# MetaFormer block, 16 images of 128 x 32 x 32: the first image taken in halves up to its first K, the second weight scale moved to round 1, the statistics of image 1 moved behind the maxima of image 0

## The reference

```python
x = x + _L0_conv_ref(_ln_c(x), w_qkv, w_out, b_out)   # attention on the normalised image
t = _to_tokens(x)
t = t + _L0_ffn_ref(_ln_t(t), Wr, br, W1, ..., Wo, bo)
...
    k = jax.nn.softmax(k, axis=-1)                    # over the 1024 pixels
    context = jnp.einsum('bhdn,bhen->bhde', k, v)
    out = jnp.einsum('bhde,bhdn->bhen', context, q)
...
    w = jax.nn.softmax(jnp.mean(x, axis=0) @ Wr + br, axis=-1)
    h = relu(_bn(x @ W1 + b1, g1, be1, m1, v1))       # per expert
    h = relu(_bn(h @ W2 + b2, g2, be2, m2, v2))
    return einsum(h @ Wo + bo, w)
```

## Time and profile before

| | us |
|---|---|
| median of 3 runs (lowest, highest) | 821.94 (819.64, 822.42) |
| profiled execution | 819.77 |
| its span | 818.0 |
| PE busy | 791.9 |
| POOL, DVE, ACT busy | 578.8, 525.6, 443.5 |

### The profile page before, as it was taken

The page is one execution under the profiler, slowest core; times in us unless marked ns, Lnnn a source line. Parts: engine busy times, 40 slices in busy tenths (PEclk is TensorE's granted clock), DMA queues, the critical chain, the costliest instruction groups (busy, mean ns, idle before and its releaser), DMA issues.

```text
span 818.0 us, 12728 instructions
## 1 busy us (share of the span) xinstructions
PE 791.9 (97%) x4186; PEld 669.9 (82%) x4186; DVE 525.6 (64%) x999; ACT 443.5 (54%) x560; POOL 578.8 (71%) x497
## 2 busy tenths in 40 slices
PE   6999999999998799999999999999999999999997
PEld 5998999999987678888888888888888888888885
DVE  4688777877865446665665656656656566565663
ACT  2576767767675554554554545545455455454542
POOL 5558788787857168667766776777777776677665
PEclk9999999999999889999999999999999999999999
DMA  7124344343342160210101201102022020110100
GB/s 240 53 79 161 123 163 147 112 170 128 131 154 103 54 231 1 78 65 13 77 26 51 77 0 77 54 23 77 1 77 77 0 77 26 51 77 0 51 26 26
DMA packets 22107, 64.52 MB, mean 79 GB/s; under 512 B 2608, under 2 KB 6840, under 8 KB 22080
## 3 DMA queue, kind: packets, MB, share of 16 engines
q1 hardware_dynamic: 22080, 64.19, 21.4%
HBM read 38.98 MB, written 25.20 MB: 78 GB/s over the span
## 4 chain that ended last, share of the span: by engine, by line
PE 64%; ACT 1%; DVE 0%; POOL 0%; POOLq 0%; issue 0%; DVEq 0%
PE psum L552 63%; PE psum L505 1%; PE psum L621 0%; POOL xn_lo L1045 0%; POOLq L83 0%; ACT h_hi L731 0%; PE psum L608 0%; DVE x_res L985 0%; DVE w_raw L928 0%; ACT xn_hi L743 0%; ACT route_all L767 0%; PE psum L584 0%; ACT feat_most L754 0%; ACT z_early L736 0%; ACT xn2T L695 0%
## 5 line engine op out<-in xcount | busy, mean ns | idle before, releaser
L912 DVE SCALAR_TENSOR_TENSOR h_lo<-psum,h_hi 128x1024 fp32r<-128x1024 f32 x128 | 156.8, 1225 | 207.4 <-ACT h_hi L731 207.4
L731 ACT ACTIVATE h_hi<-psum 128x1024 fp32r<-128x1024 f32 x128 | 131.3, 1026 | 255.9 <-PE psum L552 255.9
L1045 POOL TENSOR_TENSOR h_lo<-w_raw,h_hi 128x1024 fp32r<-128x1024 f32 x64 | 154.1, 2408 | 53.5 <-ACT h_hi L743 53.5
L552 PE MATMUL psum<-h_hi,w_hi 128*128 128x512 f32 x384 | 120.4, 395 | 1.7 <-DVE w_raw L928 0.9
L928 DVE SCALAR_TENSOR_TENSOR w_raw<-psum,minus_t,route_all 128x1024 f32<-128x1024 f32 x94 | 119.9, 1275 | 1.3 <-DMA route_all<-route_scratch 1.3
L552 PE MATMUL psum<-h_hi,w_lo 128*128 128x512 f32 x384 | 120.5, 395 | 0.0
L552 PE MATMUL psum<-h_lo,w_hi 128*128 128x512 f32 x384 | 119.5, 393 | 0.0
L1045 POOL TENSOR_TENSOR xn_lo<-w_raw,xn_hi 128x1024 fp32r<-128x1024 f32 x32 | 78.1, 2441 | 51.9 <-ACT xn_hi L743 51.9
L1045 POOL TENSOR_TENSOR xn_lo<-feat_most,xn_hi 128x1024 fp32r<-128x1024 f32 x32 | 77.2, 2413 | 51.0 <-ACT xn_hi L743 51.0
L1024 POOL TENSOR_TENSOR ln<-ln,const 128x8 f32<-128x8 f32 x32 | 52.6, 1643 | 57.6 <-DVE ln L896 57.6
L552 PEld LDWEIGHTS psum<-h_hi,w_hi 128*128 128x128 f32 x384 | 72.7, 190 | 17.5 <-issue 1.3
(11 more groups left out here) (146 smaller groups left out, 1445.1 us busy)
## 6 DMA issues: line engine op xcount, KB each, us to landing
route_all<-in_x SPq DMA_DIRECT2D x16, 512.0 KB, 3.9
x_res<-in_x SPq DMA_DIRECT2D x16, 512.0 KB, 3.3
x_scratch<-x_res SPq DMA_DIRECT2D x16, 512.0 KB, 2.8
xn_scratch<-xn SPq DMA_DIRECT2D x16, 512.0 KB, 2.6
xs_in<-xn_scratch SPq DMA_DIRECT2D x16, 512.0 KB, 4.5
x_res<-x_scratch SPq DMA_DIRECT2D x16, 512.0 KB, 3.2
out<-x_res SPq DMA_DIRECT2D x15, 512.0 KB, 2.6
route_all<-route_scratch SPq DMA_DIRECT2D x6, 512.0 KB, 6.2
```

What stands on the lines that cost most here:

```text
L552: mm = pe.matmul(dst[:, px], w[:, which, e, :], part[:, px], start=first and w is w_hi and part is hi, stop=last and part is lo, skip_grou ...
L731: nc.scalar.activation(h1_hi[r][:], z1[r], ACT.Relu).then_inc(h1_hi_done, 1)
L912: nc.vector.scalar_tensor_tensor(out=h1_lo[r][:], in0=z1[r], scalar=0.0, in1=h1_hi[r][:].bitcast(F32), op0=ALU.max, op1=ALU.subtract).then ...
L1045: nc.gpsimd.tensor_tensor(h2_lo[r][:], h2w[r], h2_hi[r][:].bitcast(F32), ALU.subtract).then_inc(h2_lo_done, 1)
```

## The change

**Loads.** `ident` is issued first, then image 0 in two halves of 512 pixels with a semaphore each, then `small_sb`: `small_sb` goes from second to fourth in the queue, and every later load is one issue later.

**Image 0.** The transposes, the copy to `xT` and the `bn_stats` of image 0 run in halves of four chunks, and so do the transposes of its normalised form, `xn_hi` and `xn_lo`. K(0) begins on the first half.

**Weights.** S1 is still spread and multiplied into W1 before round 0; the product on DVE now stands behind `xn_lo` of image 0. S2 is spread in round 1, behind K(1), and multiplied there into W2. The part of the `small_sb` chain that gives t2 stands behind the normalisation of image 0 (`second_shift`). The shifts through Wo stand behind K(0).

**Order in rounds 0 and 1.** The statistics of image 1 stand behind the maxima of image 0 and `bo_full` on DVE. The transposes of the normalised image 1 (`turn_xn`) stand behind the last `turn_e` of round 0. The high parts of the expert weights are made in the order Wo, W1, W2, where it was Wo, W2, W1.

```diff
         def _(sp):
-            sp.dma_start(x_in[0], x[0]).then_inc(in_loaded[0], 16)
+            sp.dma_start(ident[:], ident_in).then_inc(ident_loaded, 16)
+            sp.dma_start(x_in[0][:, 0:BANK], x[0][:, 0:BANK]).then_inc(x0_loaded, 16)
+            sp.dma_start(x_in[0][:, BANK:PIXELS], x[0][:, BANK:PIXELS]).then_inc(in_loaded[0], 16)
             sp.dma_start(small_sb[:], small).then_inc(small_loaded, 16)
-            sp.dma_start(ident[:], ident_in).then_inc(ident_loaded, 16)
...
                 if at(t, 0):
+                    pe.wait_ge(expert_w, 6 * 16)
+                    shifts_through_wo()
+                    turn_e(t, 0, 0)
                     shift_weights()
+                if at(t, 1):
+                    pe.wait_ge(w1_shifted, 1)
+                    pe.wait_ge(cols_done, 1)
+                    spread_scales(p_chan, S2)
...
                 if at(t, -1):
 
                     pe.wait_ge(wT_moved, 1)
-                    pe.wait_ge(cols_done, 1)
-                    spread_scales(p_late, S2)
+                    pe.wait_ge(first_cols_done, 1)
                     spread_scales(p_chan, S1)
...
+                    pe.wait_ge(norm1_first, 1)
+                    turn_part(p_tok, 128, lambda n: xnT[0][:, n, :], 0, 4).then_inc(xn0_turned, 1)
+                    pe.wait_ge(norm1_done, 1)
+                    turn_part(p_tok, 128, lambda n: xnT[0][:, n, :], 4, CHUNKS).then_inc(xnt_done, 1)
+                if b and a and not at(t, 0):
+                    turn_xn(t, q)
...
-                if at(t, -1):
-
-                    pe.wait_ge(scaled, 1)
-                    shifts_through_wo()
...
                     turn_e(t, 1, 1)
+                    if at(t, 0):
+                        turn_xn(t, q)
                     add_g(t, p, 1, 0)
                     add_g(t, p, 1, 1)
...
+                if at(t, -1):
+                    act.wait_ge(xn0_turned, 1)
+                    nc.scalar.copy(xn_hi[0][:, 0:BANK], p_tok[:, 0:BANK]).then_inc(xn0_hi_done, 1)
+                    act.wait_ge(xnt_done, 1)
+                    nc.scalar.copy(xn_hi[0][:, BANK:PIXELS], p_tok[:, BANK:PIXELS]).then_inc(xn_hi_done, 1)
+                elif a:
...
-                if at(t, -1):
-
-                    dve.wait_ge(expert_w, 6 * 16)
-                    for k, scales in ((1, p_late), (0, p_chan)):
-                        dve.wait_ge(bcast_done, 2 - k)
-                        nc.vector.tensor_tensor(flat[k], flat[k], scales, ALU.mult).then_inc(scaled, 1)
...
+                if at(t, 1):
+                    scale_weights(1)
                 if at(t, 0):
 
                     dve.wait_ge(wo_t2_done, 1)
                     nc.vector.tensor_tensor(bo_full[:], p_g[0:EXPERTS, 256:384], bo_sb[:], ALU.add).then_inc(bo_full_done, 1)
+                    halves(0, xT, 1)
+                    statistics(0, 1, LN_C_EPS)
                     dve.wait_ge(shift_done, 1)
...
-            for k, (g, v, b, m, be, s) in enumerate(((G1, V1, B1, M1, BE1, S1), (G2, V2, B2, M2, BE2, S2))):
+            for k, (g, v, s) in enumerate(((G1, V1, S1), (G2, V2, S2))):
...
+                if at(t, -1):
+                    second_shift()
```

More of the change, by code:

```diff
@@ L383, in step @@
                     turn_xn2(t)
-                if b:
+                if b and not at(t, 0):
                     turn_e(t, 0, 0)
@@ L474, in turn_xn2, with turn_xn @@
                 turn(dst, lambda n: xn2T[:, n, :]).then_inc(xn2t_done, 1)
+            def turn_xn(t, q):
+                pe.wait_ge(norm1_done, t + 2)
+                pe.wait_ge(exp_done, 2 * t + 2)
+                turn(p_tok, lambda n: xnT[q][:, n, :]).then_inc(xnt_done, 1)
             def spread_scales(dst, col):
@@ L501, in turn, with turn_part @@
                 return turn_part(dst, 128, chunk)
-            def turn_part(dst, rows, chunk):
-                for n in range(CHUNKS):
+            def turn_part(dst, rows, chunk, first=0, last=CHUNKS):
+                for n in range(first, last):
                     mm = pe.transpose(dst[0:rows, 128 * n:128 * (n + 1)], chunk(n), ident[:])
@@ L849, in step @@
                     halves(0, xT, t + 2)
-                if a:
+                if at(t, -1):
+                    dve.wait_ge(xn0_hi_done, 1)
+                    nc.vector.tensor_tensor(xn_lo[0][:, 0:BANK], p_tok[:, 0:BANK], xn_hi[0][:, 0:BANK].bitcast(F32),
+                                            ALU.subtract).then_inc(xn0_lo_done, 1)
+                    dve.wait_ge(xn_hi_done, 1)
+                    nc.vector.tensor_tensor(xn_lo[0][:, BANK:PIXELS], p_tok[:, BANK:PIXELS], xn_hi[0][:, BANK:PIXELS].bitcast(F32),
+                                            ALU.subtract).then_inc(xn_lo_done, 1)
+                    scale_weights(0)
+                elif a:
                     dve.wait_ge(xn_hi_done, t + 2)
                     nc.vector.tensor_tensor(xn_lo[q][:], p_tok, xn_hi[q][:].bitcast(F32), ALU.subtract).then_inc(xn_lo_done, 1)
-                if s and not b:
-                    halves(0, xT, t + 2)
-                if s:
+                if at(t, -2):
+                    dve.wait_ge(x0_copied, 1)
+                    for n in range(4):
+                        nc.vector.bn_stats(st[0][:, n, :], xT[:, n, :])
+                    dve.wait_ge(copy1_done, 1)
+                    for n in range(4, CHUNKS):
+                        ins = nc.vector.bn_stats(st[0][:, n, :], xT[:, n, :])
+                    ins.then_inc(stats_done[0], 1)
+                if s and not at(t, -1):
                     statistics(0, t + 2, LN_C_EPS)
```

76 lines of the change are left out of this document (49 added, 27 removed).

## The result

| | us |
|---|---|
| changed kernel, median of 7 runs (lowest, highest) | 825.03 (821.94, 827.73) |
| kernel before, 7 runs beside it | 819.64 (818.65, 822.42) |
| ratio of changed to before, 95% interval | 1.006 (1.0035 to 1.0085) |
| profiled execution, its span | 825.03, 823.2 |

The changed kernel is slower, by 0.6%: 4.9 us by the ratio, 5.4 by the medians. The median of before was 819.64 beside it and 819.1 to 820.2 in all later comparisons, not the 821.94 of the three runs that the prediction was put on. So it is luck that the predicted 825.2 lies within 0.2 us of the measured 825.03: the base was 2.3 us too high and the predicted difference of 3.3 us was 1.2 to 2.1 us too low.

What follows compares the result with a forecast made beforehand. TensorE, busy 791.9 of 818.0 us, was taken as the bound. K(1) 1.65 later, round 1 0.45 and the clock 1.2 gave 3.3 us slower: 825.2 against the median of 821.94, range 820.5 to 828.5.

Steps and rivals of the forecast that it cites:

- Start of the power: POOL's power of image 0, behind its chain on `small_sb`: starts at 10.89 instead of 11.16, 0.3 us earlier.
- the two bounds: Power of image 0: 9.95 if `small_sb` landed as before, 11.7 if it took the third load's 3.7 us.
- From the power to K(0): Opening, from POOL's power of image 0 to TensorE's K(0): 7.75 us become 6.0; K(0) 2.0 us earlier, at 16.9.
- Work moved behind K(0): TensorE in round 0: shifts through Wo now stand behind K(0), 1.9 us more work.
- What is late next: Round 0: image 1's statistics behind `bo_full` make TensorE wait 0.6 and 1.1 us; K(1) at 34.2, 1.65 us later.
- The rival in which the chain of image 1 fits: Round 0 on DVE: chain from K(0) to K(1) 15.55 us or less, no wait; 821.4 to 822.3; chance 0.20.
- Round 1: Spread of S2 between K(1) and the context: 0.45 us more, the rest filling the wait ahead of `turn_e`.
- Sum without the clock: K(1) 1.65 us later plus 0.45 us in round 1: 2.1 us slower.
- The clock: Opening: one half-speed stretch hits, partly on waits, and costs 1.2 us; bounds 0 and 3.4.
- The other thin place: End of round 0: TensorE waits 1.7 us within 4.5, where a half-speed stretch could follow, costing up to 1.7 us.

Runs made afterwards that it cites:

- both edits: Changed kernel with round 0 in its former order and the small vectors issued second; median 819.02 us, ratio to the kernel before 0.9989.
- each single edit: Changed kernel with either round 0 in its former order (median 820.54 us) or the small vectors issued second in the queue (820.71 us).

## Why the prediction came out as it did

**Start of the power: 0.3 us too good.** I had 10.89 from 3.05 us between issue and first use. POOL started at 5.57, 3.45 us after the issue at 2.12, and at 5.0 to 5.9 over the eight executions with `small_sb` fourth; the power came at 11.19, as late as before. With `small_sb` second, right behind `ident`, POOL started 2.0 to 2.8 us after the issue, in four executions. So the landing of this small load went by its place in the queue and by the execution. Of the two bounds the late one (11.7, from `ident`) was the nearer, 0.5 us off.

**From the power to K(0): right.** 6.0 predicted, 6.02 measured, with ACT's copy of image 1 ahead of the casts as the reason. K(0) 1.7 us earlier instead of 2.0.

**Work moved behind K(0): right.** 1.91.

**What is late next: right, and shown.** Waits of 0.45 and 1.07 us were predicted as 0.6 and 1.1; K(1) followed K(0) by 17.5 us, predicted 17.3. Putting the statistics back took both waits away and 1.9 us with them; taking 1.9 us of work away moved K(1) closer to K(0) by no more than 0.55. The rival in which the chain of image 1 fits is out.

**Round 1: right.** The first `turn_e` of round 2 is 2.59 us late (53.40, 50.81 before) where K(1) was 2.16: 0.43, predicted 0.45.

**Sum without the clock:** predicted 2.1, measured 2.6 (1.7 early instead of 2.0, and 0.2 in the chain). It stands unchanged up to the routing stage: 2.64 us at 255.

**The clock: right in kind, incomplete in place.** K(0) at half clock is there in two of four executions at 1.4 to 1.8 us, near the 1.2 that I took as one stretch partly on waits; in one of the two it was no fall but a late first rise. The other thin place, the waits at the end of round 0, brought none in any profile. In the profile that came with the result K(0) and round 0 had full clock, and there the excess over 2.6 lay in the routing stage, for which the prediction had said that both traces would run alike. Over the four executions of the changed kernel that stage had 17.1, 13.6, 10.2 and 17.1 us of half clock, against 13.6 in before's one.

Four profiles are few, but every execution has its mean granted clock measured. It was 0.9907 over the 15 of the changed kernel and 0.9929 over the 81 of before that were run beside the experiments; it was 0.994 or more in none of the 15 and in 28 of the 81. That is 15.4 against 11.7 us of half clock in an execution, the time ahead of the first rise not counted. So the changed kernel does spend more time at half clock, 3.7 us more. If that falls on work, half of it, 1.8 us, is what it costs; this is an estimate, and the routing stage above shows how much it depends on where the half clock falls. The version with both edits, at 0.9936, spends no more than before.

**What stays open.** By the ratios the loss is 4.5 to 4.9 us. 2.6 of it are the opening at full clock, and 1.9 to 2.3 are left, near those 1.8. K(0) at half clock makes up 1.4 to 1.8 in those executions that have it, 0.8 on average if they are half of them. That leaves about 1 us, and what the profiles show for it is the long half-clock stretch of the routing stage, which came with 2.9 us. It was there in two of four profiles of the changed kernel and not in the one of before; no run shows whether a later start of that stage makes it likelier or whether this is chance. Most executions seem to have one of the two or both: the profile with neither took 821.74 us, and of the 15 only one more lies near it (821.94), while the others took 823.35 to 827.73. The same surplus shows from the other side: each single edit lowered the median by 3.4 us or more, where its opening accounts for 1.9 and 1.3.

**The term that was mis-sized.** The forecast of the difference was 3.3, against 4.5 to 4.9. Half a microsecond of that is the opening (the landing of `small_sb` and 0.2 in the chain); the rest is the clock, priced at 1.2 in all, where 1.9 to 2.3 are left over, about 1 of them outside the two places that I had named.

## What to carry to other kernels

When a start is brought forward, ask which of its inputs is last after the edit: here the statistics of the image were ready at 9.04, and the power that needs them still started at 11.19, because the 40 KB load that had to make room for the image sat at the head of another engine's chain. Work that is moved off an opening's path lands on a stage where TensorE has no idle time, and there it costs its full length, plus the wait of whatever was queued behind it on a third engine. An opening with thinner TensorE work can also lose the clock: with a spread of eight transposes removed, K(0) came 0.7 us later and not earlier, in one execution of each kernel. And before a difference of a few microseconds is explained by one pair of profiles, the same program should be profiled again: four profiles of one kernel lay between 821.7 and 826.9 us.

## What was not expected of the hardware

Two executions of one program with the same rows ahead of K(0), to 0.02 us, differed in the clock behind it: full in one, half for 3.4 us in the other. The clock column reads 1.00 in the first microseconds of every execution, while 8 transposes take 1.94 to 2.01 us there instead of 1.09. The routing stage took 2.9 us longer with half-clock stretches of 13.6 and 3.4 us than with two of 6.8, because TensorE was busy for 16.4 us of the former and 11.4 of the latter. The kernel with 26 transposes of no use in its waits has a median of 822.34 against 824.14 (3.2 us above before instead of 4.3), which the intervals do not separate. The 40 KB load let POOL start 2.0 to 3.8 us after its issue, by its place in the queue and by the execution.
